# The first attention unit's loads issued inside the last QKV block, with the end of that block rearranged

## The chip, the cores and the metric

The kernel runs on one core of one Trainium2 chip. The metric is the device time of one execution in microseconds (us), here the median of three runs. The engines are TensorE (PE in the profile, PEld for its weight loads), VectorE (DVE), ScalarE (ACT), GpSimd (POOL) and SyncE (SP), which only issues DMAs here.

## The reference

One transformer block with adaptive modulation, on x of shape (2, 2048, 576), 16 heads of 36:

```python
mod = silu(c) @ ada_w.T + ada_b            # shift, scale, gate for attention and MLP
gate_msa, gate_mlp = tanh(gate_msa), tanh(gate_mlp)
h = modulate(rmsnorm(x, g1, D), scale_msa, shift_msa)
q, k, v = split(h @ qkv_w.T + qkv_b)       # q, k: rmsnorm per head; q also * HEAD_DIM ** -0.5
o = softmax(q @ k.T) @ v                   # per batch and head
x = x + gate_msa * (o @ proj_w.T + proj_b)
h2 = modulate(rmsnorm(x, g2, D), scale_mlp, shift_mlp)
x = x + gate_mlp * (gelu(h2 @ fc1_w.T + fc1_b) @ fc2_w.T + fc2_b)
```

## The kernel before

All work is in float32, much of it as a high and a low part for TensorE. There are two blocks of code, one after the other, with a barrier between them in which every engine waits for all others.

`qkv_phase` goes over 8 blocks of 512 tokens (number i = 2 it + r: four steps `it`, batch r), each of four tiles of 128 tokens, so 32 tiles tt = 0 to 31; the last block holds tiles 28 to 31. Per tile TensorE computes two halves of q, k, v (L606). VectorE takes them out of PSUM with the bias (L479, L481), ScalarE squares (L380), VectorE sums per head (L519), ScalarE takes the root (L384), VectorE inverts and scales (L457 to L464), TensorE transposes nine pieces (L568, `turn`), ScalarE copies the high part `tq_hi` (L390, `turned`) and VectorE the low part `tq_lo` (L470, `turned_low`). SP stores v per tile to DRAM (L240) and the two transposed parts one tile later (L226, `store_qk`). `tq_hi` and `tq_lo` exist once: `turned` waits until the stores of the tile before have landed (`tq_dma`). Beside this VectorE computes "dots" (L493), matrix-vector products of the modulation for later, by the list `DOTS`: products 0 in tile 0 of a block, none in tile 1, 1 and 2 in tile 2, 3 and 4 in tile 3. GpSimd prepares low parts of the next block (L297, L70). ScalarE takes two tanh of the gates after its last tile (L403). At the block's end SP waits until all these stores have landed (L254).

`main_phase` starts with attention: 64 units u of 512 queries for two heads; four units share the keys and values of one pair of heads and one batch. Each of SP, PE and DVE first reads a flag (`unbounded`) from SBUF and branches over code that isn't needed with this data; ScalarE and GpSimd don't. GpSimd sets constant rows of both key buffers `kT` to one (L1007) and clears `osb` (L1010). SP waits for the first memset and loads keys, queries and values of the first unit (L874, L865, L867, L883): 3 DMAs for each of four key blocks of 512, 3 and 1 for the queries, 1 for the values. Each unit has 16 steps: two score matmuls (L1385) into one of three PSUM slots, one exponential (L1039); eight steps are split by VectorE into `p_hi` (L1210) and `p_lo` (L1216) and multiplied with the split values `vx` (L1410), eight are multiplied whole (L1396, L1397). VectorE splits the values first (`split_v`, L1201, L1203). After attention come projection and MLP in the same block.

The order on every engine is written by hand, and a waiting instruction holds all behind it on its engine; DMAs of SP run through one queue per DMA engine in the order of issue. SBUF of the two phases overlaps, placed by address.

Of the kernel before, what the change touches and what calls it, by code (L numbers as in the profile page):

```python
# [78 lines left out]
def f32(ap):  # L79
    return ap.bitcast(F32)  # L80


def build(nc, xT, cT, ada, adan, adab, wqkv, qkvb, wp, pb, w1, f1b, w2, f2b, gains, outT):
# [7 lines left out]
    with ExitStack() as ctx:  # L91
# [17 lines left out]
        qkv_phase(nc, ctx, sb, ps, xT, cT, ada, adan, adab, wqkv, qkvb, pb, f1b, f2b, gains, qk_hi, qk_lo, v_s, m_s,  # L109
                  ident, ones, mod, gate_b, gain, qscale, bound, unbounded, pb_t, f2b_t, f1b_t)  # L110
        main_phase(nc, ctx, ps, qk_hi, qk_lo, v_s, m_s, l_s, oh_s, ol_s, xT, w2, wp, w1, outT, ident, ones, unbounded, mod, gate_b,
# [3 lines left out]
def qkv_phase(nc, ctx, sb, ps, xT, cT, ada, adan, adab, wqkv, qkvb, pb, f1b, f2b, gains, qk_hi, qk_lo, v_s, m_s,  # L115
# [5 lines left out]
    with ExitStack() as st:  # L121
        def sem(name):
            return ctx.enter_context(nc.semaphore("a_" + name))

        aw = sb(st, "aw", [P, 2, KC * DP])
# [28 lines left out]
        tq_hi, tq_lo = (aw[:, 0, j * 2 * D:(j + 1) * 2 * D].bitcast(F32R).rearrange("p (c n) -> p c n", c=QKC) for j in range(2))  # L154

# [25 lines left out]
        turn_mm, tqhi_done, tqlo_done, tq_dma = sem("turn_mm"), sem("tqhi_done"), sem("tqlo_done"), sem("tq_dma")  # L181
# [9 lines left out]
        with nc.Block() as block:  # L191
            @block.sync
            def _(sp):
# [28 lines left out]
                def store_qk(tt, col):  # L222

                    sp.wait_ge(tqlo_done, tt + 1)
                    for part, out in ((tq_hi, qk_hi), (tq_lo, qk_lo)):
                        sp.dma_start(out[:, bass.ds(col, P)].rearrange("(c p) n -> p c n", p=P), f32(part)).then_inc(tq_dma, 16)  # L226

                def body(it, first, last):
                    for r in range(B):
# [3 lines left out]
                        for t in range(TPB):  # L233
                            tt = TPB * (B * it + r) + t
                            if r == 1 and t == TPB - 1 and not last:
# [5 lines left out]
                                         stv[:, t % 2]).then_inc(v_dma[t % 2], 16)  # L241
                            if t > 0:
# [27 lines left out]
            def _(pool):  # L270
# [30 lines left out]
                iterate(pool, NIT, body)  # L301

# [43 lines left out]
            def _(act):  # L346
# [44 lines left out]

                def body(it, first, last):
# [7 lines left out]
                turned(NTILES - 1)  # L400
                act.wait_ge(modn_add, 2 * NIT)
                for g in (GATE_MSA, GATE_MLP):
                    act.activation(mod[:, g], mod[:, g], ACT.Tanh).then_inc(tanh_done, 1)  # L403

            @block.vector
            def _(dve):
# [95 lines left out]
                DOTS = ((0,), (), (1, 2), (3, 4))  # L502

                def body(it, first, last):
                    for r in range(B):
                        i = B * it + r
                        more = not (last and r == 1)
                        for t in range(TPB):
# [12 lines left out]
                            for m in DOTS[t]:  # L521
# [5 lines left out]
                turned_low(NTILES - 1)  # L527
# [3 lines left out]
                for j, (g, b_t) in enumerate(((GATE_MSA, pb_t), (GATE_MLP, f2b_t))):  # L531
                    dve.tensor_tensor(gate_b[:, j], mod[:, g], b_t[:].unsqueeze(2).to_broadcast([P, KC, B]),
                                      ALU.mult)

# [129 lines left out]
def main_phase(nc, ctx, ps, qk_hi, qk_lo, v_s, m_s, l_s, oh_s, ol_s, xT, w2, wp, w1, outT, ident, ones, unbounded, mod, gate_b,  # L664
# [42 lines left out]
    kT[0] = following("kT0", [PKW, 2, N], F32R)  # L707
    vp[0] = following("vp0", [P, NT, VP])
# [3 lines left out]
    qT = following("qT", [PKW, 2, 2, BLK], F32R)  # L712
# [15 lines left out]
    gated = following("gated", [P, 2, BLK])  # L728
    h_hi = following("mh_hi", [P, 2, KC, BLK], F32R)
# [4 lines left out]
    w1_raw = following("w1_raw", [P, 2, KC, P])  # L734
# [11 lines left out]
    wp_ld, kones, osb_zero = sem("wp_ld"), sem("kones"), sem("osb_zero")  # L746
    w2hi_done, w2_done, wphi_done, wplo_done = sem("w2hi_done"), sem("w2_done"), sem("wphi_done"), sem("wplo_done")
    q_ld = [sem(f"q_ld{j}") for j in range(2)]
    k_ld = [[sem(f"k_ld{j}_{c}") for c in range(C)] for j in range(B)]
    v_ld = [sem(f"v_ld{j}") for j in range(B)]  # L750
# [43 lines left out]

    def row_maxima_sync(sp):
        def load(it, r, h):
# [10 lines left out]
        for r in range(B):  # L807
# [8 lines left out]
            store(PAIRS - 1, r, 1)  # L816

    def row_maxima_tensor(pe):
        for r in range(B):
            with pe.Fori(0, PAIRS) as it:  # L820
                for h in range(2):
# [9 lines left out]
                    pe.transpose(MT, mo[:], ident[:]).then_inc(m_turn, 1)  # L831

# [755 lines left out]
```

## Time and profile before

| | |
|---|---|
| median of three runs | 2960.52 us (2960.25 to 2960.9) |
| the profiled execution | 2961.68 us |
| its span, first to last instruction | 2959.8 us |
| TensorE busy | 2900.7 us, 98% |
| VectorE busy | 1971.7 us, 67% |
| ScalarE busy | 1581.8 us, 53% |
| GpSimd busy | 220.1 us, 7% |
| mean granted TensorE clock | 0.993 of full |

Times in the rows are us from the span's start. A row of the timeline gives start, duration, engine, line, operation, output and input, the count if several follow each other, and in brackets how long the engine had been idle before it and what ended that. The windows give busy time per engine, granted clock (1.00 is 2.4 GHz, 0.50 is 1.2 GHz), busy share of the 16 DMA engines and GB/s. QKV lasts until about 467 us, attention until about 1908 us. The page's means of one instruction are 1.02 to 1.03 us for an exponential, 0.69 us for a cast to `p_hi` and 1.22 us for a `p_lo`.

### The profile page before, as it was taken

The page shows a single profiled execution, that of the slowest core. Times are in us where ns is not written, and L with a number is a line of the kernel's source. Part 1 is how long each engine was busy: PE and PEld are TensorE (multiplying, and loading weights), DVE is VectorE, ACT ScalarE, POOL GpSimd, SP SyncE. Part 2 cuts the span into 40 slices and gives each one's busy share as a digit, 9 for nine tenths or more (in the row PEclk, how much of TensorE's full clock was granted, in tenths as well). Part 3 has the DMA queues.
Part 4 walks back from the last instruction along what each step waited for, and adds up shares of the span by engine and source line. Part 5 has one row for each costly group of instructions (what it writes and reads, how often), then busy time and mean ns, then how long its engine had stood idle before and what let it go on. Part 6 is the DMA issues. An engine that isn't in the chain of part 4 may idle for free.

```text
span 2959.8 us, 35431 instructions
## 1 busy us (share of the span) xinstructions
PE 2900.7 (98%) x13080; PEld 2194.8 (74%) x13080; DVE 1971.7 (67%) x2687; ACT 1581.8 (53%) x1926; POOL 220.1 (7%) x153
## 2 busy tenths in 40 slices
PE   8999996999999999999999999999999999999998
PEld 7999994666666666666666666688888888888886
DVE  5777775899888888888888887844343342424332
ACT  3333324677676676776776766634344343434342
POOL 3232301000000000000000000090000000000000
PEclk9999997999999999999999999999999999999999
DMA  5465545222222222322223223342222222322121
GB/s 211 150 194 160 177 142 157 63 82 76 75 83 76 74 72 75 86 77 79 79 62 86 73 76 95 116 139 89 72 85 72 80 77 91 102 77 88 41 68 45
DMA packets 238407, 282.85 MB, mean 96 GB/s; under 512 B 34912, under 2 KB 143968, under 8 KB 237344
## 3 DMA queue, kind: packets, MB, share of 16 engines
q1 hardware_dynamic: 232992, 270.18, 30.0%
q10 hardware_dynamic: 5248, 10.49, 1.0%
q8 instruction: 100, 1.64, 0.2%
q14 instruction: 67, 0.55, 0.1%
HBM read 195.66 MB, written 84.67 MB: 95 GB/s over the span
## 4 chain that ended last, share of the span: by engine, by line
PE 82%; DVE 1%; ACT 1%; SPq 0%; DMA 0%; issue 0%; POOL 0%; DVEq 0%; ACTq 0%; POOLq 0%
PE ps L1385 16%; PE ps L1410 16%; PE ps L1469 15%; PE ps L1452 15%; PE ps L1397 13%; PE ps L1428 4%; PE ps L1396 2%; ACT gated L1092 1%; DVE x L1267 0%; SPq L874 0%; DVE x L1271 0%; DVE x L1273 0%; DVE w_lo L1261 0%; DMA kT<-qk_hi_scratch 0%; POOL kT L1007 0%
## 5 line engine op out<-in xcount | busy, mean ns | idle before, releaser
L1039 ACT ACTIVATE p_r<-ps 128x1024 f32<-128x1024 f32 x512 | 491.9, 1024 | 423.6 <-PE ps L1385 423.6
L1216 DVE TENSOR_TENSOR p_lo<-p_r,p_hi 128x1024 fp32r<-128x1024 f32 x512 | 613.2, 1218 | 0.0
L1385 PE MATMUL ps<-qT,kT 110*128 110x512 f32 x2048 | 573.6, 397 | 21.2 <-DMA qT<-m_scratch 19.8
L1385 PEld LDWEIGHTS ps<-qT,kT 110*128 110x128 f32 x2048 | 382.8, 190 | 155.4 <-issue 51.4
L1039 ACT ACTIVATE prob<-ps 128x1024 f32<-128x1024 f32 x512 | 483.5, 1030 | 2.1 <-PE ps L1385 1.6
L1396 PE MATMUL ps<-prob,vp 128*64 128x512 f32 x1024 | 453.1, 595 | 0.0
L1397 PE MATMUL ps<-prob,vp 128*37 128x512 f32 x1024 | 451.7, 594 | 0.0
L1338 DVE TENSOR_TENSOR a_lo<-act,a_hi 128x512 fp32r<-128x512 f32 x144 | 102.7, 713 | 518.9 <-ACT a_hi L1082 518.9
L1210 DVE CAST p_hi<-p_r 128x1024 fp32r<-128x1024 f32 x512 | 350.1, 694 | 135.0 <-ACT p_r L1039 133.6
L1469 PE MATMUL ps<-a_hi,w 128*128 128x512 f32 x1296 | 415.6, 393 | 0.6 <-DVE a_lo L1338 0.6
L1410 PE MATMUL ps<-p_hi,vx 128*128 128x512 f32 x1024 | 404.1, 395 | 0.1
L1410 PE MATMUL ps<-p_lo,vx 128*128 128x512 f32 x1024 | 403.2, 394 | 0.0
L1080 ACT ACTIVATE act<-ps,f1b_t 128x512 f32<-128x512 f32 x144 | 99.2, 689 | 503.8 <-PE ps L1452 503.8
L1397 PEld LDWEIGHTS ps<-prob,vp 128*37 128x37 f32 x1024 | 111.5, 114 | 247.7 <-issue 247.7
L1452 PE MATMUL ps<-mh_hi,w_hi 128*128 128x512 f32 x720 | 282.2, 392 | 1.2 <-DVE w_lo L1261 1.2
L1469 PEld LDWEIGHTS ps<-a_hi,w 128*128 128x128 f32 x1296 | 243.3, 188 | 53.6 <-DVE a_lo L1338 1.0
L1469 PE MATMUL ps<-a_lo,w 128*128 128x512 f32 x720 | 280.6, 390 | 0.0
L1452 PE MATMUL ps<-mh_hi,w_lo 128*128 128x512 f32 x720 | 280.1, 389 | 0.0
L1410 PEld LDWEIGHTS ps<-p_hi,vx 128*128 128x128 f32 x1024 | 192.5, 188 | 45.6 <-issue 1.6
L1410 PEld LDWEIGHTS ps<-p_lo,vx 128*128 128x128 f32 x1024 | 193.6, 189 | 43.1
L1452 PE MATMUL ps<-mh_lo,w_hi 128*128 128x512 f32 x576 | 224.7, 390 | 0.0
L606 PE MATMUL ps<-w_hi,h_hi 128*128 128x432 f32 x640 | 182.2, 366 | 4.6 <-DVE h_hi L70 4.6
(165 smaller groups left out, 3612.5 us busy)
## 6 DMA issues: line engine op xcount, KB each, us to landing
w_raw<-w SPq DMA_DIRECT2D x144, 320.0 KB, 2.9
qk_hi_scratch<-aw SPq DMA_DIRECT2D x32, 576.0 KB, 3.1
qk_lo_scratch<-aw SPq DMA_DIRECT2D x32, 576.0 KB, 4.4
kT<-qk_hi_scratch SPq DMA_DIRECT2D x128, 144.0 KB
qT<-qk_hi_scratch SPq DMA_DIRECT2D x128, 144.0 KB
v_scratch<-stv SPq DMA_DIRECT2D x32, 512.0 KB, 2.6
vp<-v_scratch SPq DMA_DIRECT2D x16, 1024.0 KB, 9.1
xb<-xT SPq DMA_DIRECT2D x8, 1280.0 KB, 10.0
```

The costliest lines, as they stand in the source:

```text
L606: mm = pe.matmul(ps[:, q, 0:PIECE], a[:, r, k, cols], w[:, k, q * PIECE:(q + 1) * PIECE], start=k == 0 and n == 0, stop=k == KF and n == 1)
L1039: act.activation(out, ps[:, 2 * slot:2 * slot + 2, :].rearrange("p a b -> p (a b)"), ACT.Exp).then_inc(exp_done, 1)
L1210: dve.tensor_copy(p_hi[:, q % HIGHS], p_r[:, j]).then_inc(phi_done, 1)
L1216: dve.tensor_tensor(p_lo[:, j], p_r[:, j], f32(p_hi[:, q % HIGHS]), ALU.subtract).then_inc(plo_done, 1)
L1338: dve.tensor_tensor(a_lo[:, slot], act32[:, slot], f32(a_hi[:, slot]), ALU.subtract).then_inc(alo_done, 1)
L1385: mm = pe.matmul(ps[:, 2 * (entry % RING) + h, :], kT[r][:, h, kt * P:(kt + 1) * P], qT[:, u % 2, h], start=True, stop=True)
L1396: pe.matmul(OA[0:64], vp[r][:, kt, 0:64], prob[:, j, 0:BLK], start=False, stop=False)
L1397: pe.matmul(OBK[64:VW], vp[r][:, kt, 64:VW], prob[:, j, BLK:2 * BLK], start=False, stop=False).then_inc(fv_mm, 1)
L1410: mm = pe.matmul(out, vx[r][:, j, h], part[:, h * BLK:(h + 1) * BLK], start=j == 0 and n == 0, stop=j == NS - 1 and n == 1)
L1428: mm = pe.matmul(proj_bank(i, m), w[:, k, m * P:(m + 1) * P], a[:, k], start=k == 0 and n == 0, stop=k == KF and n == 1)
L1452: mm = pe.matmul(ps[:, 5 + slot, :], w[:, slot, c], a[:, i % 2, c], start=c == 0 and n == 0, stop=c == KF and n == 1)
L1469: mm = pe.matmul(ps[:, m, :], w, a[:, slot], start=k == 0 and n == 0, stop=k == FC - 1 and n == len(parts) - 1)
```

## The change

- A class `FirstUnit` owns the first key buffer, first value buffer and the query buffer, placed at the base of free SBUF; in QKV the tiles `xb`, `tmp`, `h_hi` are placed first so that these buffers lie on them (on both slots of `xb`, on `tmp` and on the first piece of the even block's `h_hi`).
- In the last block, behind the V store of tile 29, SP issues all loads of the first unit, in the order keys 0, queries, keys 1 to 3, values (17 DMAs), after waits for the stores of tiles 0 to 27, for GpSimd's last low part and for the memset of the constant key rows. That memset is now issued by GpSimd at the end of its QKV work.
- Tile 31 is transposed into a buffer of its own (`last_hi`, `last_lo`, in the space of the dots' weights); its stores come last on SP, behind the waits for the V stores. SP no longer waits for their landing there but in attention, after the loads of the second unit's queries.
- In the last block the dots are taken in tile 28 (0, 1, 2) and tile 29 (3, 4). ScalarE's tanh and VectorE's gate products come ahead of tile 31's high and low copy.
- In attention GpSimd clears `osb` first and sets then only the second key buffer's rows; VectorE waits for `osb` in unit 1 instead of at the start. The MLP's `w1_raw` is placed elsewhere. In the branch that isn't taken, a reload of the maxima is added.

```diff
+    def load(self, sp):
+        for c in range(NIT):
+            cols = slice(c * BLK, (c + 1) * BLK)
+            for j, part in enumerate((self.qk_hi, self.qk_lo, self.qk_hi)):
+                sp.dma_start(f32(self.kT[j * HD:(j + 1) * HD, :, cols]),
+                             part[D:D + 2 * HD, cols].rearrange("(h d) n -> d h n", h=2)).then_inc(self.k_ld[c], 16)
+            if c == 0:
+                for j, part in enumerate((self.qk_hi, self.qk_hi, self.qk_lo)):
+                    sp.dma_start(f32(self.qT[j * HD:(j + 1) * HD, 0]),
+                                 part[0:2 * HD, cols].rearrange("(h d) n -> d h n", h=2)).then_inc(self.q_ld[0], 16)
+                self.load_m(sp, self.q_ld[0])
+        sp.dma_start(self.vp[:], self.v_s[0:NT, :, 0:VP].rearrange("t p c -> p t c")).then_inc(self.v_ld, 16)
...
+                            if last and r == 1 and t == 1:
+                                sp.wait_ge(zero_dma, 16)
+                                sp.wait_ge(tq_dma, 32 * (NTILES - TPB))
+                                sp.wait_ge(hlo_done, B * NIT)
+                                sp.wait_ge(first_unit.kones, 1)
+                                first_unit.load(sp)
                             if t > 0:
                                 store_qk(tt - 1, P * (TPB * it + r * NT + t - 1))
...
-                store_qk(NTILES - 1, B * N - P)
-                sp.wait_ge(zero_dma, 16)
-                sp.wait_ge(tq_dma, 32 * NTILES)
                 for j in range(2):
                     sp.wait_ge(v_dma[j], 16 * NTILES // 2)
+                store_qk(NTILES - 1, B * N - P)
...
                 iterate(pool, NIT, body)
+                pool.wait_ge(hlo_done, B * NIT)
+                pool.memset(f32(first_unit.kT[96:PKW]), 1.0).then_inc(first_unit.kones, 1)
...
+                def turned_last():
+                    act.wait_ge(turn_mm, NTILES)
+                    act.activation(last_hi.rearrange("p c n -> p (c n)"), TP, ACT.Copy).then_inc(tqhi_done, 1)
...
-                turned(NTILES - 1)
                 act.wait_ge(modn_add, 2 * NIT)
                 for g in (GATE_MSA, GATE_MLP):
                     act.activation(mod[:, g], mod[:, g], ACT.Tanh).then_inc(tanh_done, 1)
+                turned_last()
...
+                DOTS_LAST = ((0, 1, 2), (3, 4), (), ())
...
-                            for m in DOTS[t]:
+                            for m in (DOTS if more else DOTS_LAST)[t]:
...
-            sp.wait_ge(kones, 1)
-            load_k(0, 0)
-            load_q(0)
-            load_v(0)
-            for c in range(1, C):
-                load_k(0, c)
-
             for u in range(NU):
                 g, c = u // C, u % C
                 if u + 1 < NU:
                     load_q(u + 1)
                 if u == 0:
+                    sp.wait_ge(first_unit.tq_dma, 32 * B * NT)
                     sp.wait_ge(kones, 2)
...
-            for r in range(B):
-                pool.memset(f32(kT[r][96:PKW]), 1.0).then_inc(kones, 1)
-                pool.wait_ge(kones, r + 1)
             for j in range(2):
                 pool.memset(osb[j][:], 0.0).then_inc(osb_zero, 1)
+                pool.wait_ge(osb_zero, j + 1)
+            pool.memset(f32(kT[1][96:PKW]), 1.0).then_inc(kones, 1)
...
-            dve.wait_ge(osb_zero, 2)
             split_v(0)
```

## Rows read from the trace of the kernel before

**Rows 1.** Windows: us, busy by engine (instructions), clock, DMA share, GB/s.

```profile
448.00:479.00 31.00, 3.30 (x17) 2.66 (x16) 8.80 (x17) 5.13 (x7) 8.01 (x4) 0.58 0.48 145
520.00:620.00 100.00, 99.94 (x438) 64.61 (x433) 87.63 (x116) 68.65 (x76) 7.39 (x4) 1.00 0.28 78
```

**Rows 2.** Waits of TensorE and SP at the hand-over: total, times, longest.

```profile
PE ps L1385 <- DMA qT<-m_scratch: 19.8, 1, 19.8
PE ps L1385 <- DMA kT<-qk_hi_scratch: 1.4, 1, 1.4
...
SPq L254 <- DMA qk_lo_scratch<-aw: 3.7, 1, 3.7
```

**Rows 3.** Timeline, the last tile of QKV (tile 31).

```profile
450.08 1.35 DVE L519 TENSOR_REDUCE ssb<-w_raw 128x32 f32<-128x1152 f32 x1 [1.23 <-ACT w_raw L380]
451.35 0.75 DVE L493 CUSTOM_DVE_ANT_0 w_raw<-aw,c_b 128x576 f32<-128x576 f32 x1
...
456.57 2.18 PE L568 MATMUL ps<-ident,stq 128*128 128x128 f32 x9 [7.90 <-DVE stq L464]
459.30 1.13 ACT L390 ACTIVATE aw<-ps 128x1152 fp32r<-128x1152 f32 x1 [7.59 <-DMA qk_lo_scratch<-aw]
...
460.46 1.36 DVE L470 TENSOR_TENSOR aw<-ps,aw 128x1152 fp32r<-128x1152 f32 x1 [3.94 <-ACT aw L390]
...
462.26 0.61 SPq L226 DMA_DIRECT2D qk_lo_scratch<-aw  x1
```

**Rows 4.** The chain of waits after the barrier: start, duration, what.

```profile
467.15 3.52 POOL kT L1007
...
470.68 0.40 SPq L874
...
473.91 4.19 SPq L874
```

**Rows 5.** TensorE's branch (first, last start us) and the timeline of unit 0.

```profile
L1473 PEldq COMPARE_BRANCH  x1: 215/215/215, 468.1 to 468.1; - x1
...
478.56 3.78 PE L1385 MATMUL ps<-qT,kT 110*128 110x512 f32 x8 [19.81 <-DMA qT<-m_scratch]
484.22 1.29 DVE L1210 CAST p_hi<-p_r 128x1024 fp32r<-128x1024 f32 x2
485.03 7.68 ACT L1039 ACTIVATE prob<-ps 128x1024 f32<-128x1024 f32 x8 [1.44 <-PE ps L1385]
487.76 0.40 PE L1410 MATMUL ps<-p_hi,vx 128*128 128x512 f32 x1
```

**Rows 6.** Timeline, tiles 29 to 31: V store of 29, copy of 29, evacuation.

```profile
424.90 0.34 SPq L240 DMA_DIRECT2D v_scratch<-stv  x1
...
437.97 1.11 ACT L390 ACTIVATE aw<-ps 128x1152 fp32r<-128x1152 f32 x1
...
447.73 0.76 DVE L479 TENSOR_TENSOR stq<-ps,bias 128x576 f32<-128x576 f32 x1 [2.24 <-PE ps L606]
```

**Rows 7.** Windows in which a V store, key loads, and q and k stores run.

```profile
484.00:490.00 6.00, 6.00 (x20) 4.65 (x21) 6.00 (x8) 4.97 (x6) 0.00 (x0) 0.73 0.80 225
425.70:427.20 1.50, 1.50 (x9) 1.43 (x9) 1.10 (x1) 1.39 (x2) 0.00 (x0) 1.00 0.87 350
443.50:446.00 2.50, 2.50 (x15) 2.39 (x14) 1.92 (x3) 0.00 (x0) 0.00 (x0) 1.00 1.15 347
```

**Rows 8.** Timeline: GpSimd beside VectorE in an earlier tile, and tile 26.

```profile
101.96 2.66 POOL L259 TENSOR_TENSOR tmp<-tmp 128x512 f32<-128x512 f32 x2 [11.26 <-ACT tmp L317]
103.61 1.04 DVE L457 TENSOR_SCALAR rt<-rt 128x32 f32<-128x32 f32 x1
392.69 1.70 POOL L70 TENSOR_TENSOR h_hi<-tmp,h_hi 64x512 fp32r<-64x512 f32 x1
397.23 0.17 DVE L457 TENSOR_SCALAR rt<-rt 128x32 f32<-128x32 f32 x1
399.50 1.20 PE L568 MATMUL ps<-ident,stq 128*128 128x128 f32 x9 [0.49 <-DVE stq L464]
```

More of the change, by code:

```diff
@@ L112, in build, with __init__, sem, load_m @@
                    gain, f1b_t)
-def qkv_phase(nc, ctx, sb, ps, xT, cT, ada, adan, adab, wqkv, qkvb, pb, f1b, f2b, gains, qk_hi, qk_lo, v_s, m_s,
+class FirstUnit:
+    def __init__(self, nc, ctx, qk_hi, qk_lo, v_s, m_s):
+        def sem(name):
+            return ctx.enter_context(nc.semaphore("m_" + name))
+        base = (nc.sbuf_base + 63) // 64 * 64
+        self.qk_hi, self.qk_lo, self.v_s, self.m_s = qk_hi, qk_lo, v_s, m_s
+        self.kT = nc.alloc_sbuf_tensor_at("kT0", [PKW, 2, N], F32R, offset=base)
+        self.vp = nc.alloc_sbuf_tensor_at("vp0", [P, NT, VP], F32, offset=base + 8 * N)
+        self.qT = nc.alloc_sbuf_tensor_at("qT", [PKW, 2, 2, BLK], F32R, offset=base + 8 * N + 4 * NT * VP)
+        self.size = 8 * N + 4 * NT * VP + 16 * BLK
+        self.k_ld = [sem(f"k_ld0_{c}") for c in range(NIT)]
+        self.q_ld = [sem(f"q_ld{j}") for j in range(2)]
+        self.v_ld, self.kones, self.tq_dma = sem("v_ld0"), sem("kones"), sem("tq_dma")
+    def load_m(self, sp, loaded):
+        sp.dma_start(f32(self.qT[3 * HD:PKW, 0]), self.m_s[0:4, 0:BLK].rearrange("(h j) n -> j h n", h=2)).then_inc(loaded, 16)
+    def load(self, sp):
[10 more added lines that the diff above has]
+        sp.dma_start(self.vp[:], self.v_s[0:NT, :, 0:VP].rearrange("t p c -> p t c")).then_inc(self.v_ld, 16)
@@ L123, in sem @@
             return ctx.enter_context(nc.semaphore("a_" + name))
+        xb = sb(st, "xb", [P, 2, KC, BLK])
+        tmp = sb(st, "tmp", [P, KC, BLK])
+        h_hi = sb(st, "h_hi", [P, 2, KC, BLK], F32R)
+        h_lo = sb(st, "h_lo", [P, 2, KF, BLK], F32R)
+        w_hi = sb(st, "w_hi", [P, KC, NP * PIECE], F32R)
         aw = sb(st, "aw", [P, 2, KC * DP])
@@ L154, in qkv_phase @@
         tq_hi, tq_lo = (aw[:, 0, j * 2 * D:(j + 1) * 2 * D].bitcast(F32R).rearrange("p (c n) -> p c n", c=QKC) for j in range(2))
+        last_hi, last_lo = (aw[:, 1, j * 2 * D:(j + 1) * 2 * D].bitcast(F32R).rearrange("p (c n) -> p c n", c=QKC) for j in range(2))
         raw = [w_raw[:],
@@ L224, in store_qk @@
                     sp.wait_ge(tqlo_done, tt + 1)
-                    for part, out in ((tq_hi, qk_hi), (tq_lo, qk_lo)):
+                    final = isinstance(tt, int) and tt == NTILES - 1
+                    for part, out in ((last_hi if final else tq_hi, qk_hi), (last_lo if final else tq_lo, qk_lo)):
                         sp.dma_start(out[:, bass.ds(col, P)].rearrange("(c p) n -> p c n", p=P), f32(part)).then_inc(tq_dma, 16)
@@ L706, in main_phase @@
     kT, vp = [None, None], [None, None]
-    kT[0] = following("kT0", [PKW, 2, N], F32R)
-    vp[0] = following("vp0", [P, NT, VP])
+    kT[0], vp[0], qT = first_unit.kT, first_unit.vp, first_unit.qT
+    here[0] += first_unit.size
     kT[1] = following("kT1", [PKW, 2, N], F32R)
@@ L728, in main_phase @@
     gated = following("gated", [P, 2, BLK])
+    w1_raw = following("w1_raw", [P, 2, KC, P])
     h_hi = following("mh_hi", [P, 2, KC, BLK], F32R)
@@ L745, in main_phase @@
     w2_ld = [sem(f"w2_ld{j}") for j in range(4)]
-    wp_ld, kones, osb_zero = sem("wp_ld"), sem("kones"), sem("osb_zero")
+    wp_ld, kones, osb_zero = sem("wp_ld"), first_unit.kones, sem("osb_zero")
     w2hi_done, w2_done, wphi_done, wplo_done = sem("w2hi_done"), sem("w2_done"), sem("wphi_done"), sem("wplo_done")
-    q_ld = [sem(f"q_ld{j}") for j in range(2)]
-    k_ld = [[sem(f"k_ld{j}_{c}") for c in range(C)] for j in range(B)]
-    v_ld = [sem(f"v_ld{j}") for j in range(B)]
+    q_ld = first_unit.q_ld
+    k_ld = [first_unit.k_ld, [sem(f"k_ld1_{c}") for c in range(C)]]
+    v_ld = [first_unit.v_ld, sem("v_ld1")]
     s_mm, exp_done, fv_mm, rv_mm = sem("s_mm"), sem("exp_done"), sem("fv_mm"), sem("rv_mm")
```

30 lines of the change are left out of this document (18 added, 12 removed).

## The prediction

> **What bounds the kernel now.** I read the stage table first. In the attention stretch TensorE works 99.94 of 100 us, but between 448 and 479 us it works only 3.30 of 31 us [rows 1]. So attention, and the MLP behind it, only move with the moment TensorE starts them, and the place to gain is the hand-over from QKV to attention. The waits name its pieces: 19.8 us for the first queries and 1.4 us for the second key block [rows 2]. The last transposes had waited 7.90 us more [rows 3]. The chain of waits shows what filled the 19.8 us: SP waits 3.7 us for the last tile's stores to land [rows 2], then GpSimd's memset of 3.52 us, then loads that are issued from 470.68 us on [rows 4]; the first score matmul starts at 478.56 us [rows 5]. A saving there reaches the end one for one, as nothing else limits after the first unit.
>
> **Part 1, stores of the last tile no longer awaited.** In the last tile VectorE ends its low part at 460.46 + 1.36 = 461.82 us and SP has issued both stores at 462.26 + 0.61 = 462.87 us [rows 3]; the block ends at about 467.1 us, just ahead of the memset [rows 4]. After the change SP waits in that place only for V stores, which are long down, and the block can end some 0.3 us after the last issue. Worth 467.1 - 463.2 = 3.9 us if the issue stays where it is. The wait reappears on SP ahead of unit 0's load for the other batch; behind it are only keys wanted four units later, so it costs nothing.
>
> **Part 2, the loads and the memset leave the hand-over.** Between block end and first score are now 478.56 - 467.1 = 11.4 us. What stays is reading the flag and branching: PE's branch ends at 468.1 + 0.2 = 468.3 us [rows 5], so 1.2 us, and I allow 0.2 us more. No row shows when PE would have been ready for the first score; SP, behind its own branch, stood until the memset ended at 470.67 us [rows 4], so up to that point an engine may still have been fetching code. Gain 10.0 us, bounds 7.9 to 10.2.
>
> **Part 3, the 1.4 us gap.** With all keys present ScalarE's exponentials run without the 1.44 us hole [rows 5]. They pace unit 0 (7.68 us for 8), so the half-rate clock of the first scores costs nothing. But VectorE has little room: its first p_hi cast was at 484.22 us and its split parts were used from 487.76 us on [rows 5]; a chain that keeps its distance from the first score while the matmuls come 1.44 us earlier is late by some 0.5 us (two casts and a low part, 2.4 us by the page's means of 0.69 and 1.22, leave 1.1 us of the 3.5, and the following parts come more slowly than the matmuls). The distance stays only if the V split starts late, see part 5. I take 1.0 us, bounds 0 to 1.4.
>
> **Part 4, what the loads push back in QKV.** SP issues 17 more DMAs behind the V store of tile 29 (424.90 + 0.34 us [rows 6]). Eight took 470.68 to 473.91 us, so 0.40 us each, and the one behind the V load stood 4.19 us [rows 4]. The V load is now last, at 425.3 + 16 x 0.40 = 431.7 us, and so the one that stands is the high store of tile 28: it is out at 436.5 us and the low one at 437.1 us, where V's scratch store for tile 30 queues behind. The data matter more. Key and query transfers of 144 KB moved at 225 GB/s with engines 0.80 busy, stores of 512 B pieces at 347 GB/s [rows 7]: 15 x 147 KB / 225 = 9.8 us, 1.05 MB of V / 347 = 3.0 us (its source pieces are 512 B as well), and 1.18 MB of tile 28 = 3.4 us, after the V store of tile 29 that holds the engines until 427.2 us [rows 7]. With 0.5 us to land, T = 427.2 + 9.8 + 3.0 + 3.4 + 0.5 = 443.9 us. ScalarE's copy of tile 29 waits for T; it now starts at 437.97 us [rows 6]. Behind it lie VectorE's low part, 1.1 + 1.4 us, the next evacuation, 1.2 us, and the scaling chain, 2.3 us (397.23 to 399.5 us [rows 8]), 6.0 in all, which TensorE's turn just ahead of the evacuation at 447.73 us [rows 6] needs: T may be 441.4 us at no cost. So the tail slips by 2.5 us. Bounds for T: 440.5 us, if all 4.44 MB ran at 347 GB/s, no slip; 447.5 us at 200 GB/s for the 3.26 MB of loads, a slip of 6.
>
> The Trainium skill (DMA: Bandwidth & Descriptors, "Why a DMA increments its semaphore by 16 and not by 1") lets a transfer use the largest count of engines up to 16 that divides both slow dimensions. For 36 rows that is 12 of 16, always the lowest-numbered, a share of 0.75 beside the 0.80 of the row. By 16 engines the sum would have no slip and end 2.4 us earlier.
>
> **Part 5, the memset beside VectorE.** It now follows GpSimd's last low part, 392.69 + 1.70 = 394.4 us, and ends near 397.9 us. Does VectorE care? At 103.61 us a tiny tensor_scalar that takes 0.17 us elsewhere took 1.04 us and ended with GpSimd's adds (101.96 + 2.66) [rows 8]: it stood until GpSimd was free. The same instruction stands at 397.23 us, so it would wait 0.7 us, and TensorE's turn, which already waits 0.49 us for that chain, starts 0.75 us later [rows 8]. Cost 0.75 us, bounds 0 and 1.5 (both tensor_scalars of the chain). The other memset, for the second batch, now comes after two small ones at the start of the attention block, right where VectorE wants to split the first V. Its copies have one source, as the tensor_scalar; I hold them back until the memset ends, which keeps VectorE's distance to the first score about as before, and that is why part 3 is 1.0 us.
>
> The Trainium skill (SBUF — State Buffer, Terms, "shared port pair") says the pair is held for a whole instruction and the loser blocks. It speaks against putting either memset there; without it the sum would be 1.2 us better.
>
> **Part 6, dots and tanh.** Two dots and their sum leave the last tile's path: 1.6 us between the reduction and the low part (451.35 us on, 0.75 us each and a read) [rows 3]. They go to tiles 28 and 29, where VectorE waits 2.24 us per tile for TensorE [rows 6] (that row is tile 31's, others alike); tile 28 has two dots more, 1.6 us, tile 29 two, so nothing there. If that cover were gone, 1.6 us. The tail without slip: low part of tile 30 at 451.45 to 452.8, its scaling chain 2.3 us (397.23 to 399.5 [rows 8]) to about 455.0, nine transposes at half clock 2.18 us [rows 3] to 457.2, copy 1.13, low part 1.36, end 459.7 us instead of 461.82. The separate buffer removes ScalarE's wait of 7.59 us until 459.30 [rows 3]; what is late next is the transposes. Tanh and its table load move into ScalarE's idle time ahead of them. Gain 2.1 us, and with the slip of 2.5 us the end is at 462.0 to 462.2, 0.3 us later than now.
>
> **The sum.** 3.9 + 10.0 + 1.0 + 2.1 - 2.5 - 0.75 = 13.8 us. The profiled execution lasts 2961.68 us (2959.8 us span and 1.9 us around it), 1.2 us over the median of 2960.52; I take the saving from the median: **2946.7 us**.
>
> **The rivals.**
> (a) No slip: the transfers overlap better. For: busy share 1.15 of the stores shows spare; against: 0.80 in the loads. Gain 16.3, 2944.2 us.
> (b) The queue is slower, or SP stands longer, slip 6 us or the end of the block still waits for descriptors or landing (3.9 us not gained): gain 10, 2950.5 us. For: none of the rows shows a block end right behind a DMA issue. This is also the case that the change only half does what it says.
> (c) Slower than before: the loads crawl in the midst of stores, and ScalarE, VectorE and TensorE stand behind one store of tile 28. Each us of T beyond 441.4 costs one; the saving is used up at T = 441.4 + 16.3 = 457.7 us, which needs the 3.3 MB to take 27 us, 120 GB/s, and 5.9 us more, at 100 GB/s, gives 2966 us. Against: 225 GB/s.
> (d) The hole is filled by another wait: VectorE's V split or a code fetch delays the first unit, so that 5 to 9 us of the 13.8 remain and it lies within 0.2% or just beyond: 2954 us.
>
> **How the numbers follow.** Forecast (slip 1 to 4 us) 0.50; (a) 0.20; (b) 0.20; (d) 0.06; (c) 0.04. The range takes in (a) with 1.7 us of luck, and (b) with 1.5 us more: 2942.5 to 2952. 0.2%, 5.9 us, is about what a measurement can tell from no change. Faster: all but (c) and half of (d), 0.93; same 0.04; slower 0.03.
>
> **What would show it.** TensorE's idle time ahead of the first score should be 5 to 7 us instead of 19.8, and the wait for the second key block gone. Part 4: ScalarE's copy of tile 29 released by the DMA at 443 to 445 us; if it starts near 438 us, (a). Part 5: the tensor_scalar near 397 us takes 0.9 us and the transposes wait 1.2 us. Part 1: SP's drain behind SP's last store is short. Wrong it would be if loads take over 20 us, or if the first V split starts over 4 us after the first score.

## The result, and the profile after

The changed kernel takes 2949.34 us (median of 6 runs, 2948.27 to 2949.77) against 2961.59 us of the kernel before (median of 6 runs, three of them those of the table above, 2960.25 to 2962.86): a ratio of 0.9957, with a 95% interval of 0.9947 to 0.9967. The gain is 12.3 us by the medians; the spans of the two profiled executions differ by 2959.8 - 2946.6 = 13.2 us. Forecast were 13.8 us and a time of 2946.7 us, with a range of 2942.5 to 2952.0 us.

The hand-over first. These are rows of the timeline of the changed kernel: start, duration, what, and in brackets the idle time before and what ended it.

```profile
458.96 2.18 PE L624 MATMUL ps<-ident,stq 128*128 128x128 f32 x9 [5.82 <-DVE stq L513]
461.18 1.13 ACT L439 ACTIVATE aw<-ps 128x1152 fp32r<-128x1152 f32 x1 [3.79 <-PE ps L624]
462.34 1.36 DVE L557 TENSOR_TENSOR aw<-ps,aw 128x1152 fp32r<-128x1152 f32 x1 [3.20 <-ACT aw L439]
464.21 0.60 SPq L264 DMA_DIRECT2D qk_lo_scratch<-aw  x1
465.22 1.11 POOL L1063 MEMSET osb<- 101x512 f32 x2 [67.18 <-POOLq L228]
466.39 3.51 POOL L1065 MEMSET kT<- 14x4096 f32 x1
466.81 3.37 DVE L1256 CAST vx<-vp 128x512 fp32r<-128x512 f32 x1 [3.11 <-issue]
466.97 4.87 PE L1441 MATMUL ps<-qT,kT 110*128 110x512 f32 x12 [5.83 <-issue]
468.20 3.77 ACT L1094 ACTIVATE p_r<-ps 128x1024 f32<-128x1024 f32 x4 [5.89 <-PE ps L1441]
471.83 5.65 ACT L1094 ACTIVATE prob<-ps 128x1024 f32<-128x1024 f32 x6
```

TensorE's idle time ahead of the first score fell from 19.81 us [rows 5] to 5.83 us, and it now waits for no DMA there ("issue"). The last low part ends at 462.34 + 1.36 = 463.70 us, 1.88 us later than before [rows 3]. The last store is issued by 464.81 us, and the next block begins 0.41 us behind it. The first score starts 1.75 us after that, where it took 11.4 us [rows 4, 5]. The second unit's first score is at 489.01 us, before at 501.83 us: 12.8 us of the 13.2 are there at the end of unit 0, the other 0.4 us come later and I have not traced them. In the middle of attention TensorE works 99.94 of 100 us in both kernels ([rows 1] and the last of these windows of the changed kernel: us, busy by engine, granted clock, DMA share, GB/s).

```profile
429.00:431.00 2.00, 2.00 (x12) 1.91 (x11) 1.97 (x4) 0.00 (x0) 0.00 (x0) 1.00 0.73 219
431.00:433.00 2.00, 2.00 (x12) 1.90 (x11) 1.90 (x7) 0.00 (x0) 0.00 (x0) 1.00 0.82 202
433.00:435.00 2.00, 2.00 (x12) 1.92 (x11) 1.28 (x1) 0.00 (x0) 0.00 (x0) 1.00 0.73 204
...
427.90:445.70 17.80, 17.80 (x97) 16.98 (x96) 8.68 (x16) 1.40 (x2) 0.00 (x0) 1.00 0.94 264
...
448.00:467.00 19.00, 3.83 (x22) 2.86 (x20) 11.24 (x20) 5.13 (x7) 1.66 (x3) 0.64 0.62 194
490.00:590.00 100.00, 99.94 (x436) 66.81 (x435) 87.12 (x115) 73.25 (x81) 3.69 (x2) 1.00 0.29 86
```

The second thing is what the change costs inside QKV: the new memset in tile 26, the loads on SP, and ScalarE's copy of tile 29 behind them. Timeline of the changed kernel:

```profile
394.52 3.52 POOL L345 MEMSET kT<- 14x4096 f32 x1
395.01 1.35 DVE L519 TENSOR_TENSOR aw<-ps,aw 128x1152 fp32r<-128x1152 f32 x1
397.31 0.77 DVE L506 TENSOR_SCALAR rt<-rt 128x32 f32<-128x32 f32 x1
400.19 1.20 PE L624 MATMUL ps<-ident,stq 128*128 128x128 f32 x9 [1.07 <-DVE stq L513]
...
433.17 0.63 SPq L148 DMA_DIRECT2D vp<-v_scratch  x1
433.85 5.74 SPq L264 DMA_DIRECT2D qk_hi_scratch<-aw  x1
439.63 1.91 SPq L264 DMA_DIRECT2D qk_lo_scratch<-aw  x1
441.59 1.83 SPq L278 DMA_DIRECT2D v_scratch<-stv  x1
...
446.20 1.13 ACT L434 ACTIVATE aw<-ps 128x1152 fp32r<-128x1152 f32 x1 [7.42 <-DMA qk_lo_scratch<-aw]
447.36 1.36 DVE L519 TENSOR_TENSOR aw<-ps,aw 128x1152 fp32r<-128x1152 f32 x1 [7.20 <-ACT aw L434]
```

The tensor_scalar takes 0.77 us instead of 0.17 [rows 8] and ends at 398.08 us, as the memset does (398.04 us). The copy of tile 29 waits 7.42 us for the store of tile 28 and starts at 446.20 us, where it started at 437.97 us [rows 6].

### The profile page after: what moved, and what is told of

The parts are those of the page before. It is cut to its first block, busy times and chain, and to the rows that moved or that the text cites. A ratio compares the mean times of both kernels' runs of the same rounds, so it can differ in the third digit from the quotient of the medians.

```text
span 2946.6 us, 35430 instructions
## 1 busy us (share of the span) xinstructions
PE 2899.7 (98%) x13080; PEld 2192.2 (74%) x13080; DVE 1974.3 (67%) x2687; ACT 1581.6 (54%) x1926; POOL 220.6 (7%) x153
## 4 chain that ended last, share of the span: by engine, by line
PE 82%; DVE 1%; ACT 1%; issue 0%; DVEq 0%; ACTq 0%
PE ps L1441 16%; PE ps L1466 16%; PE ps L1525 15%; PE ps L1508 15%; PE ps L1453 14%; PE ps L1484 4%; PE ps L1452 2%; ACT gated L1147 1%; DVE x L1322 0%; DVE x L1326 0%; DVE x L1328 0%; DVE w_lo L1316 0%; ACT p_r L1094 0%; DVE tmp L1325 0%; PE ps L1496 0%
```

## The experiments

All edits are made to the changed kernel. Whole traces are shifted by up to 1 us against that of the changed kernel before the region in question begins, so moments are compared after setting the start of GpSimd's last run of low parts (388.10 us in the changed kernel, 387.08 to 388.99 us in all) to the same value; such moments are called aligned. Of each run the table has the median, its ratio to the kernel before on the same chip with the interval, the aligned start of the second unit's first score, and the length of unit 0. The kernel before takes 2961.7 to 2962.4 us in these sessions. The changed kernel itself ran again (e11, below), and its copy of tile 29 came 0.6 us later than the first time; in e3 and e2, whose edits come after it, 0.55 and 1.0 us later. The first trace is thus the earliest of four, and differences under 1 us behind that copy are not told apart by one trace.

| kernel | median us (runs) | ratio (95%) | unit 1 aligned | unit 0 |
|---|---|---|---|---|
| changed | 2949.34 (6) | 0.9957 (0.9947 to 0.9967) | 489.0 | 22.04 |
| e1 late loads | 2954.97 (10) | 0.9977 (0.9967 to 0.9987) | 494.9 | 23.93 |
| e2 await stores | 2952.84 (7) | 0.9969 (0.9957 to 0.9980) | 493.8 | 22.37 |
| e3 dots back | 2950.26 (5) | 0.9959 (0.9945 to 0.9973) | 491.2 | 21.96 |
| e4 values first | 2948.18 (4) | 0.9951 (0.9935 to 0.9968) | 488.7 | 22.05 |
| e5 store first | 2950.31 (4) | 0.9958 (0.9942 to 0.9975) | 490.1 | 21.94 |
| e6 memset twice | 2953.42 (9) | 0.9972 (0.9962 to 0.9982) | 494.6 | 22.01 |
| e7 spread | 2945.18 (4) | 0.9942 (0.9926 to 0.9959) | 485.7 | 21.99 |
| e8 spread, memsets | 2946.23 (4) | 0.9946 (0.9929 to 0.9962) | 486.3 | 22.62 |
| e9 first memset later | 2944.94 (5) | 0.9942 (0.9928 to 0.9955) | 485.1 | 22.02 |
| e10 memsets placed | 2944.45 (5) | 0.9941 (0.9927 to 0.9954) | 484.6 | 21.54 |
| e11 changed again | 2949.76 (5) | 0.9958 (0.9945 to 0.9972) | 489.6 | 22.04 |

**Loads back in attention (e1).** SP issues the 17 loads at the start of attention again; the memset, the last tile's own buffer, the dots and the stores stay as changed.

```diff
...
-                                sp.wait_ge(first_unit.kones, 1)
-                                first_unit.load(sp)
...
+            first_unit.load_k(sp, 0)
+            first_unit.load_q(sp)
+            first_unit.load_v(sp)
+            for c in range(1, C):
+                first_unit.load_k(sp, c)
```

> The changed kernel with the first unit's loads issued at the start of attention, in the old order (keys 0, queries, values, keys 1 to 3); its tail, dots and memset stay. Theory (the early loads pay for themselves, net of the slip they cause in QKV): without them ScalarE's copy of tile 29 starts near 438.7 us instead of 446.2, VectorE ends tile 31 near 460.5 us instead of 463.7, but the first score waits for its queries until about 470.7 us instead of 466.97 and the hole before the second key block is back; unit 1 starts near 494 us instead of 489.0, so about 5 us slower than the changed kernel and 8 us faster than the kernel before. Rival (the loads were worth their full 10 us and the slip is not theirs): the copy of tile 29 stays near 446 us and unit 1 starts at 497 us or later, gain 4 us or less.

Timeline of e1:

```profile
439.35 1.11 ACT L429 ACTIVATE aw<-ps 128x1152 fp32r<-128x1152 f32 x1
...
471.58 3.78 PE L1441 MATMUL ps<-qT,kT 110*128 110x512 f32 x8 [13.12 <-DMA qT<-m_scratch]
...
476.94 3.36 PE L1441 MATMUL ps<-qT,kT 110*128 110x512 f32 x7 [1.57 <-DMA kT<-qk_hi_scratch]
```

The slip in QKV is gone (no wait at the copy of tile 29), and TensorE waits 13.12 us for the queries instead. Unit 1 starts 5.9 us later than with the loads in QKV. So the loads' place is worth some 6 us net (5.3 us against the repeat e11), and the rest of the change keeps 7.1 us against the kernel before (501.83 + 0.11 for the alignment - 494.87).

**The stores awaited again (e2).** One wait is put back at the block's end.

```diff
                 store_qk(NTILES - 1, B * N - P)
+                sp.wait_ge(tq_dma, 32 * NTILES)
```

> The changed kernel, but SP again waits in QKV until the stores of the last tile have landed. Theory (part 1 of the sum, 3.9 us): QKV's end moves from 465.2 to 469.1 us and unit 1 starts 3.9 us later, near 492.9 us; about 9 us faster than the kernel before. Rival (the barrier waits for the queue anyway, through the drain): no difference to the changed kernel, unit 1 at 489.0 us.

Timeline of e2:

```profile
464.34 0.60 SPq L264 DMA_DIRECT2D qk_lo_scratch<-aw  x1
469.17 1.11 POOL L1064 MEMSET osb<- 101x512 f32 x2 [71.95 <-POOLq L228]
470.55 3.75 PE L1442 MATMUL ps<-qT,kT 110*128 110x512 f32 x8 [9.27 <-issue]
```

From the last issue to the next block are 469.17 - 464.94 = 4.23 us, against 0.41 us without the wait. The price of the wait is 3.8 us. Unit 1 is 4.8 us later; 1.0 us of that is an earlier difference, the later copy of tile 29. The first score comes 1.38 us after the block's start here, against 1.75 us, and unit 0 is 0.33 us longer, so these two cancel: GpSimd's memset keeps its distance to the block's start, so its end lies 0.36 us further behind the first score.

**Dots back in the last tiles (e3).**

```diff
-                DOTS_LAST = ((0, 1, 2), (3, 4), (), ())
+                DOTS_LAST = ((0,), (), (1, 2), (3, 4))
```

> The changed kernel with the dots in their old places (tiles 28, 30, 31). Theory (the two dots of tile 31 lie on the path even behind the slip; those of tile 30 are hidden by VectorE's wait of 7.2 us): unit 1 starts 1.6 us later, near 490.6 us. Rival (the slip covers the dots, so moving them is worth nothing): 489.0 us as in the changed kernel.

Timeline of e3, then of the changed kernel, from the reduction to the low part:

```profile
455.59 1.35 DVE L575 TENSOR_REDUCE ssb<-w_raw 128x32 f32<-128x1152 f32 x1 [1.23 <-ACT w_raw L424]
...
458.53 1.35 DVE L519 TENSOR_TENSOR aw<-ps,aw 128x1152 fp32r<-128x1152 f32 x1
```

```profile
454.15 1.35 DVE L575 TENSOR_REDUCE ssb<-w_raw 128x32 f32<-128x1152 f32 x1 [1.23 <-ACT w_raw L424]
455.42 1.35 DVE L519 TENSOR_TENSOR aw<-ps,aw 128x1152 fp32r<-128x1152 f32 x1
```

2.94 us against 1.27 us: the dots cost 1.67 us in that place. The aligned unit 1 is 2.2 us later, of which 0.55 us stood there before the reduction. The medians, taken on different chips, show only 0.9 us, which their intervals can't tell from 1.6 or from nothing; the rows carry this verdict.

**The memset doubled (e6).** GpSimd sets the constant rows twice, one after the other.

```diff
                 pool.wait_ge(hlo_done, B * NIT)
+                pool.memset(f32(first_unit.kT[96:PKW]), 1.0).then_inc(zero_done, 1)
+                pool.wait_ge(zero_done, 2)
                 pool.memset(f32(first_unit.kT[96:PKW]), 1.0).then_inc(first_unit.kones, 1)
```

> The changed kernel with GpSimd's memset of the key buffer's constant rows done twice, one behind the other, at the end of its QKV work. Theory (VectorE's small tensor_scalar stands until GpSimd is done): the tensor_scalar near 397.3 us lasts until about 401.6 us instead of 398.1, the transposes start near 403.7 us instead of 400.2, and all later work and the end come 3.5 us later than in the changed kernel. Rival (the 0.6 us longer wait in the changed kernel has another cause, no lock): no more than 0.2 us later.

Timeline and windows of e6:

```profile
397.11 3.51 POOL L347 MEMSET kT<- 14x4096 f32 x1
397.51 3.14 DVE L512 TENSOR_SCALAR rt<-rt,qscale 128x16 f32<-128x16 f32 x1
402.10 2.18 PE L626 MATMUL ps<-ident,stq 128*128 128x128 f32 x9 [4.00 <-DVE stq L515]
...
402.00:405.00 3.00, 2.90 (x12) 2.84 (x13) 1.77 (x4) 1.85 (x2) 0.00 (x0) 0.50 0.36 146
405.00:406.00 1.00, 1.00 (x6) 0.95 (x5) 1.00 (x2) 0.68 (x2) 0.00 (x0) 0.80 0.22 86
```

The tensor_scalar that the forecast names, 128x32, ends in the gap between the two memsets (0.77 us, as in the changed kernel). The next one, 128x16, of 0.23 us, takes 3.14 us and ends with the second memset (400.65 against 400.62 us). TensorE waits 4.00 us instead of 1.07. So far that is the theory's size. But unit 1 is 5.5 us later (4.1 us by the medians, on different chips), and the forecast had 3.5. The granted clock is 0.50 behind that wait (402 to 405 us), and the V store of tile 29 is 4.5 us later, aligned: 2.9 us of waiting and some 1.5 us of half clock. The last 1.1 us appear at the landing of tile 28's store, where the same kernel differs by as much from run to run. That a memset holds VectorE is shown; its price was under-forecast, by about what the half clock adds.

**Where the slip comes from: values first (e4), store first (e5).** In e4 the V load, in the changed kernel last of the 17, is issued first. SP then issues tile 28's high store without standing. If SP's standing at the issue made the slip, it would be gone.

```diff
+        sp.dma_start(self.vp[:], self.v_s[0:NT, :, 0:VP].rearrange("t p c -> p t c")).then_inc(self.v_ld, 16)
         for c in range(NIT):
...
-        sp.dma_start(self.vp[:], self.v_s[0:NT, :, 0:VP].rearrange("t p c -> p t c")).then_inc(self.v_ld, 16)
```

> The changed kernel with the value load first among the 17 instead of last, so that the DMA which stands behind it on SP is a key load and not the store of tile 28. Theory (the slip is the data in the queues ahead of the store: the copy of tile 29 starts when 3.3 MB of loads and the store have passed): the copy of tile 29 starts between 444.5 and 446.5 us, unit 1 within 1.5 us of 489.0 us. Rival (the slip is SP standing 5.7 and 1.9 us in the two stores of tile 28 behind the value load): the copy starts near 442 us and unit 1 near 485.5 us.

Timeline of e4:

```profile
435.52 0.41 SPq L264 DMA_DIRECT2D qk_hi_scratch<-aw  x1
435.97 2.38 SPq L264 DMA_DIRECT2D qk_lo_scratch<-aw  x1
...
446.06 1.13 ACT L434 ACTIVATE aw<-ps 128x1152 fp32r<-128x1152 f32 x1 [7.03 <-DMA qk_lo_scratch<-aw]
```

The high store is out at 435.9 us instead of 439.6 and the low one at 438.4 us instead of 441.5, and the copy of tile 29 starts at 446.06 instead of 446.20 us (445.84 us aligned). The rival had 442 us. SP's standing isn't the cause; what is left is the data ahead of the store in the queues.

In e5 the stores of tile 28 go ahead of the loads.

```diff
                             if t > 0:
                                 store_qk(tt - 1, P * (TPB * it + r * NT + t - 1))
+                                if last and r == 1 and t == 1:
...
+                                    first_unit.load(sp)
```

> The changed kernel with the 17 loads issued behind the store of tile 28 instead of ahead of it. Theory (data in the queues; whichever store comes behind 13 us of loads is late): the copy of tile 29 starts right behind its square, near 438.7 us, but the store of tile 29 now lands near 454 us and the copy of tile 30 waits for it; VectorE ends tile 31 near 463.5 us and unit 1 starts within 1 us of 489.0 us. Rival (only the stand of the store behind the value load counts): no copy waits, VectorE ends tile 31 near 460.5 us and unit 1 starts near 485.8 us.

Timeline of e5:

```profile
439.10 1.11 ACT L434 ACTIVATE aw<-ps 128x1152 fp32r<-128x1152 f32 x1
...
441.44 6.67 SPq L278 DMA_DIRECT2D v_scratch<-stv  x1
...
455.78 1.13 ACT L434 ACTIVATE aw<-ps 128x1152 fp32r<-128x1152 f32 x1 [4.59 <-DMA qk_lo_scratch<-aw]
```

The copy of tile 29 no longer waits; that of tile 30 does, and unit 1 is 1.1 us later than in the changed kernel, 0.1 us outside what was expected. The slip moves with the loads to the next store behind them.

**Loads spread over three tiles (e7).** Keys 0 to 2 go behind the V store of tile 28, queries and keys 3 behind that of tile 29, values behind that of tile 30.

```diff
+                            if last and r == 1 and t == 0:
...
+                                for c in range(3):
+                                    first_unit.load_k(sp, c)
+                            if last and r == 1 and t == 1:
+                                sp.wait_ge(tq_dma, 32 * (NTILES - TPB))
+                                first_unit.load_q(sp)
+                                first_unit.load_k(sp, 3)
+                            if last and r == 1 and t == 2:
+                                first_unit.load_v(sp)
```

> The changed kernel with the loads spread over three tiles: key blocks 0 to 2 behind the V store of tile 28, queries and key block 3 behind that of tile 29, values behind that of tile 30. Theory (each piece fits between two stores, so no store lands late): no copy waits for its store, the copy of tile 29 starts near 438.7 us, VectorE ends tile 31 near 460.5 us instead of 463.7, unit 1 starts near 485.8 us instead of 489.0: 3.2 us faster than the changed kernel. Rival (spread loads disturb three tiles instead of one): a copy waits in each of tiles 28 to 30 and the gain is under 1 us.

Timeline of e7:

```profile
427.24 1.13 ACT L442 ACTIVATE aw<-ps 128x1152 fp32r<-128x1152 f32 x1 [0.57 <-DMA qk_lo_scratch<-aw]
...
438.57 1.11 ACT L442 ACTIVATE aw<-ps 128x1152 fp32r<-128x1152 f32 x1
...
463.54 5.79 PE L1449 MATMUL ps<-qT,kT 110*128 110x512 f32 x14 [5.86 <-issue]
```

Of 7.42 us of waiting at one copy 0.57 us at another are left, and the first score is 3.3 us earlier, aligned. That is the whole slip of the changed kernel, measured: 3.3 us, and 3.9 us against its repeat e11. Nothing of a slip is left in e7: its copy of tile 31 starts at 457.87 us aligned, and in e1, which has no loads in QKV, at 457.86 us.

**The memsets.** In e8 (e7 with both memsets moved) the first is made to wait for a scaling of VectorE, the second for the fourth part of the V split.

```diff
                 pool.wait_ge(hlo_done, B * NIT)
+                pool.wait_ge(scale_done, NTILES - 6)
                 pool.memset(f32(first_unit.kT[96:PKW]), 1.0).then_inc(first_unit.kones, 1)
...
+            pool.wait_ge(v_split, 4)
             pool.memset(f32(kT[1][96:PKW]), 1.0).then_inc(kones, 1)
```

> The spread loads, and both memsets moved: the first waits until VectorE has scaled tile 25, the second until VectorE has split the first values. Theory: the tensor_scalar near 397.3 us takes 0.17 us again and the transposes behind it start near 399.6 us; the first cast of the values takes 0.42 us instead of 3.37 and VectorE is no longer late in unit 0; together 0.7 to 1.2 us faster than with the spread loads alone, unit 1 near 484.8 us. Rival (the memset then meets another VectorE operation and blocks that instead): no gain over the spread loads alone.

Timeline of e8:

```profile
466.18 4.68 DVE L1275 CAST p_hi<-p_r 128x1024 fp32r<-128x1024 f32 x2
466.20 3.51 POOL L1075 MEMSET kT<- 14x4096 f32 x1 [2.97 <-DVE vx L1268]
```

The first edit did nothing: the scaling it names was over, and the memset stood at its old place. The second moved the memset off the V split and onto the first p_hi casts: two of them take 4.68 us instead of 1.29. Unit 0 takes 22.62 us instead of 21.99: the move costs 0.6 us. In both places it meets a copy of VectorE.

In e9 (e7 again) the first memset waits one scaling further (`NTILES - 5`), and the second is left alone.

> The spread loads with the first memset alone moved: GpSimd waits for the 27th scaling (the one that ended at 400.1 us in the changed kernel), so that the memset no longer meets the tensor_scalar at 397.3 us. Theory (the lock costs 0.6 us of TensorE's time there): the tensor_scalar takes 0.17 us, the transposes behind it wait 0.5 us instead of 1.1, and unit 1 starts 0.6 us earlier than with the spread loads alone (counted from the start of GpSimd's last low part), near 484.9 us. Rival (the memset meets the next tile's work instead): the same as with the spread loads alone, or later.

Timeline of e9:

```profile
397.56 0.17 DVE L515 TENSOR_SCALAR rt<-rt 128x32 f32<-128x32 f32 x1
...
399.84 1.20 PE L633 MATMUL ps<-ident,stq 128*128 128x128 f32 x9 [0.47 <-DVE stq L522]
399.90 3.52 POOL L354 MEMSET kT<- 14x4096 f32 x1 [5.18 <-DVE stq L522]
```

The tensor_scalar is at 0.17 us and TensorE's wait at 0.47 us again, as before the change [rows 8]. Unit 1 is 0.6 us earlier than in e7; the medians (0.24 us apart, on different chips) can't show that. The later memset also holds back the first loads, and the copies of tiles 28 and 29 wait 2.10 and 0.34 us for their stores; the tail doesn't move by it.

In e10 (e9 and this) the second memset is put first in attention, ahead of the clearing of `osb`.

```diff
+            pool.memset(f32(kT[1][96:PKW]), 1.0).then_inc(kones, 1)
+            pool.wait_ge(kones, 2)
             for j in range(2):
                 pool.memset(osb[j][:], 0.0).then_inc(osb_zero, 1)
                 pool.wait_ge(osb_zero, j + 1)
-            pool.memset(f32(kT[1][96:PKW]), 1.0).then_inc(kones, 1)
```

> As the kernel above, and in attention GpSimd sets the second key buffer's rows first and clears its two small tiles after that. Theory (VectorE's first value cast stands until that memset ends, whenever it starts, and is what makes VectorE late in unit 0): the memset ends 1.2 us earlier, the value split and the first casts of unit 0 with it, the hole of 0.4 to 0.5 us in ScalarE's exponentials shrinks to under 0.2 us, and unit 0 takes 0.3 to 0.5 us less, 21.6 us from first score to unit 1. Rival (the small memsets then block the casts of the first unit): unit 0 takes 22.0 us as before or more.

Timeline of e10:

```profile
461.43 3.51 POOL L1071 MEMSET kT<- 14x4096 f32 x1 [58.11 <-POOLq L229]
463.01 2.20 DVE L1266 CAST vx<-vp 128x512 fp32r<-128x512 f32 x1 [3.11 <-issue]
```

Nearly half of the memset now runs while VectorE is still behind its branch. The first V cast is blocked for 1.8 us instead of 3, and unit 0 takes 21.54 us. This is the fastest kernel of the study, 17.3 us under the kernel before and 5.3 us under the changed kernel on the same chip (e11):

> The changed kernel itself, once more on the chip of the two kernels above, to set them against it. Theory: its time and the places of its first score and unit 1 repeat within 1 us, counted from the start of GpSimd's last low part (388.1 us in its first trace), and the two kernels above come out 3.5 to 5 us faster than it. Rival: the gain of the spread loads was a difference between executions, and they are within 1 us of each other.

e11 is the changed kernel unedited. It gave 2949.76 us and, aligned, a copy of tile 29 at 446.8 us and unit 1 at 489.6 us, both 0.6 us later than in its first trace.

## Why the prediction was right, point by point

Aligned moments and waits against the terms of the sum:

| step | forecast | measured | from |
|---|---|---|---|
| part 1, stores not awaited | 3.9 | 3.8 | 4.2 us at the block's end before, 0.41 after; e2 |
| part 2, block end to first score | 10.0 | 9.7 | 11.4 before, 1.75 after |
| part 3, unit 0 | 1.0 | 1.2 | 23.27 before, 22.04 after |
| part 6, rest of the tail | 2.1 | 2.1 | low part ends in e7 as worked out |
| part 4, slip | -2.5 | -3.3 | e7; -3.9 by the repeat e11 |
| part 5, memset in QKV | -0.75 | -0.6 | 1.07 against 0.49 us; e9 |
| sum | 13.8 | 12.9 | unit 1: 12.8 by the traces, 12.9 aligned |

**Parts 1 and 2** held. The block ends 0.4 us after the last issue (forecast 0.3), and 1.75 us pass until the first score (forecast 1.4, of which 0.2 us were a mere allowance). The doubt whether TensorE would be ready that early is settled: it is, within 1.75 us, and within 1.38 us in e2, where the engines stood 3.8 us longer at the block's end. What it does in them the profile doesn't show ("issue"); that VectorE, which also reads the flag and branches, starts at 466.81 us beside it, while GpSimd, which doesn't branch, starts at 465.22 us, speaks for flag and branch. No run here took the branch away.

**Part 3.** The hole in the exponentials is gone: ten of unit 0's run from 468.20 to 477.48 us without one, and 0.47 us of idle time come ahead of the eleventh. VectorE's V split was held back as foretold: the first cast takes 3.37 us instead of 0.42 and ends 0.28 us behind the memset. That this costs at least 0.5 us is now measured by e10, which removes part of it: unit 0 is 0.5 us shorter (21.54 against 22.04 us), and that is what was missing to the full 1.4 us and a little more.

**Part 4 is where the sum was off.** The sign was a copy of tile 29 at 443 to 445 us, from a T of 443.9 us. The V store of tile 29 was 0.7 us later, for the memset and the traces' shift, so 444.6 us stood to be compared with 446.20 us. Where the 1.6 us lie can be read from windows that begin at 427.9 us (in brackets those of the repeat e11, aligned). The bytes are counted off in the order of issue, as the windows don't tell one transfer from another:

- The step "Key and query transfers of 144 KB moved at 225 GB/s" [the first row of rows 7] held: the first 2.2 MB moved in 10.0 us at 222 GB/s (9.6 us at 226), forecast 9.8 us. In the six microseconds of the rows above, in which these loads ran nearly alone, they moved at (219 + 202 + 204) / 3 = 208 GB/s.
- The step "1.05 MB of V / 347" was mis-sized. The next 1.05 MB took 3.6 us at 284 GB/s (4.0 us at 261) instead of 3.0 us. The 1.2 MB behind it took 3.45 us at 341 GB/s (3.5 us at 340), forecast 3.4.
- The V store of tile 30 was put at nothing, as merely queued behind. From 427.9 us to the copy's start the queues moved 18.3 us x 266 GB/s = 4.87 MB, in e11 4.98, in e2 4.95 and in e3 4.84 MB, against 4.44 MB of the sum and 4.96 MB with the 0.52 MB of that store. So nearly all of it had moved too when the landing was reported, and 0.75 us (1.3 us) passed beyond the 0.5 us to land of the sum. These 0.5 us rested on no row, and no run here tells the store's bytes from a longer landing.

Of the 1.6 us only 0.8 became slip, 3.3 us instead of 2.5, because the room behind the copy had been sized too small. The T that costs nothing is 446.20 - 3.3 = 442.9 us, by e11 446.82 - 3.9 = 442.9 us as well, and the prediction's 441.4 us is 442.1 with the same 0.7 us. From the copy to the transposes pass 451.94 - 446.20 = 5.74 us instead of 6.0, and the V store of tile 31 is issued 1.01 us behind the start of these transposes, where it was 1.34 us before (447.54 and 448.88 us).

The other half of the step was right: it isn't SP's standing (e4), the slip goes with the data to whichever store comes next (e5), and it can be had for nothing where the same data are spread over three tiles that each have slack (e7). SP stood longer than the 4.19 us that I carried over, 5.74 and 1.91 us, at no cost.

The Trainium skill (DMA: Bandwidth & Descriptors, "Why a DMA increments its semaphore by 16 and not by 1") gives such loads 12 of the 16 engines; the measured shares of 0.73, 0.82 and 0.73 lie about that 0.75, and the rival that leaned on a better overlap, (a), did not come.

**Part 5.** The forecast wait of 1.2 us was 1.07 us. e6 shows the mechanism by doubling it and e9 by removing it. Only tensor_scalars and casts of VectorE were seen held by a memset: the low part at 395.01 us (two sources, one of them PSUM) takes its usual 1.35 us in the midst of it, and in e6 the reciprocal at 397.12 us its usual 0.35 us beside the second one. The Trainium skill (SBUF — State Buffer, "SBUF: two separate sides") says that the pair is an exclusive lock for the whole instruction, and that an operation with two SBUF inputs is only held by a GpSimd operation that reads SBUF; in this trace the tensor_scalar, whose end falls on the memset's, agrees with the first. A dot, which has two SBUF inputs, agrees with the second: at 393.37 us one takes 1.72 us instead of 0.75 beside GpSimd's last tensor_tensor (until 394.47 us), and it takes the same 1.72 us in the kernel before, where no memset follows.

**Part 6** held to 0.2 us where it can be read without the slip. The tail without slip was worked out to end at 459.7 us, with the memset's 0.75 us at 460.45; in e7 the last low part ends at 458.88 + 1.36 = 460.24 us (its trace is shifted by only 0.04 us against the kernel before). The 2.1 us in the table are this agreement, not a reading of their own. e3 gives 1.67 us for the dots, 1.6 were forecast. Tiles 28 and 29 hid them: VectorE still waits 1.59 and 2.17 us there for TensorE's halves.

**The rivals.** (a), no slip: refuted by 446.20 us, but e7 shows that it was to be had, at 2945.2 us. (b), a slip of 6 us or 3.9 us not gained at the block's end: the slip was 3.3 us (3.9 in the repeat) and the block end short, so neither came in full; but the measured median, 2949.34 us, lies nearer to its 2950.5 than to the forecast of 2946.7 us, by the larger slip and by the two points that follow. (c) would have needed 100 to 120 GB/s; the loads had 222. (d), a new wait in the first unit: the V split waits, but for 0.5 us.

The medians give 12.3 us and the spans 13.2. The profiled execution of the changed kernel, 2948.48 us, lies 0.9 us under its own median, while that of the kernel before lies 0.1 us over its median of six. The repeat e11, with its later copy of tile 29, reaches unit 1 12.3 us earlier than the kernel before (501.94 against 489.61 us aligned), which is the medians' gain; so the change is worth some 12 us rather than 13. I took the saving from the median of three, 2960.52 us, which turned out 1.1 us low; with 2961.59 us the same sum would have given 2947.8 us.

## What to carry to other kernels

Loads that are pulled ahead into a dense stage cost the bytes they put between a store and the engine that waits for its landing: so count these bytes in front of each such store, and cut them into pieces that fit the slack of each tile (3.3 us lost in one piece, none in three). A GpSimd memset is not free beside VectorE: look which copies of VectorE it falls on, and put it where VectorE works on other things or waits.

## What the runs showed of the hardware that was not expected

- A stall of TensorE inside a dense stage can cost more than its own length. In e6 the wait of 4.00 us was followed by a granted clock of 0.50 from 402 us to some 405.5 us, nine transposes took 2.18 instead of 1.20 us, and 2.9 us of added waiting made 4.5 us at the V store of tile 29. In the changed kernel a wait of 3.53 us at tile 30 left the transposes at 1.20 us; in its repeat e11 the wait there was 4.11 us and they took 2.18 us; the copy of tile 31 was 0.6 us later there, no more than that of tile 29.
- At the first scores the clock was back in the first unit: in the changed kernel they start at 466.97 us after 5.83 us of idle time, the granted clock is 0.50 from 467 to 470 us, with TensorE busy all the time, and full from 471 us on:

```profile
470.00:471.00 1.00, 1.00 (x4) 0.45 (x2) 0.89 (x3) 1.00 (x3) 0.00 (x0) 0.76 0.75 266
471.00:472.00 1.00, 0.84 (x3) 0.30 (x2) 0.90 (x2) 1.00 (x3) 0.00 (x0) 1.00 0.59 135
```

- The issue of one DMA stood for 2.64 us (e4) to 7.20 us (e2) behind the V load on SP, in the changed kernel 5.74 us and in its repeat 6.45 us, while in the changed kernel the loads of 36 rows took 0.3 to 0.7 us each, mostly 0.4. What sets the length no run here separates.
